# Edge attention over sorted edges: two small per-chunk tables kept on chip, and the broadcast row of relative node numbers carried as 16-bit floats

## What is computed

```python
q = (h @ Wq + bq).reshape(n, HD, HEADS) * scaling
k = (h @ Wk + bk).reshape(n, HD, HEADS)
v = (h @ Wv + bv).reshape(n, HD, HEADS)
s = jnp.einsum('edh,edh->eh', q[rows], k[cols])
m = jax.ops.segment_max(s, rows, num_segments=n)
e = jnp.exp(s - m[rows])
z = jax.ops.segment_sum(e, rows, num_segments=n)
attn = e / z[rows]
out = jax.ops.segment_sum(attn[:, None, :] * v[cols], rows, num_segments=n)
```

## Time and profile before

| | |
|---|---|
| median of 3 runs | 13238.97 us (13223.25 to 13242.68) |
| the profiled execution | 13243.9 us, its span 13242.3 us |
| PE busy | 6677.3 us (50%) |
| DVE busy | 6328.2 us (48%) |
| POOL busy | 6040.3 us (46%) |
| ACT busy | 2226.2 us (17%) |
| granted PE clock, mean | 0.736 |

### The profile page before, as it was taken

One profiled execution on the slowest core, in us unless ns is written; L12 is line 12 of the kernel. 1 busy time (PEld: TensorE's weight loads), 2 busy tenths in 40 slices (PEclk: granted clock), 3 DMA queues, 4 the chain that ended last, 5 costly groups with the idle time before them and its releaser, 6 DMA issues. The chain is left out here.

```text
span 13242.3 us, 124947 instructions
## 1 busy us (share of the span) xinstructions
PE 6677.3 (50%) x26695; PEld 4426.6 (33%) x26696; DVE 6328.2 (48%) x12364; ACT 2226.2 (17%) x4818; POOL 6040.3 (46%) x6038
## 2 busy tenths in 40 slices
PE   4647777777777659989996000000024200000399
PEld 2325555555555535555554000000013100000277
DVE  5855565656665757777777233333332100005133
ACT  1114444444443101111110000000000000000122
POOL 1215444444443045444444666666631477772300
PEclk8768898998998878998997555555555555555699
DMA  1136555555554211111112455545531111111100
GB/s 66 50 105 184 180 183 176 183 181 180 182 183 148 74 56 36 32 38 32 32 36 67 148 177 170 177 168 170 175 123 50 47 9 9 9 9 43 26 16 16
DMA packets 583830, 1307.39 MB, mean 99 GB/s; under 512 B 206400, under 2 KB 354069, under 8 KB 553239
## 3 DMA queue, kind: packets, MB, share of 16 engines
q0 software_dynamic: 296736, 704.79, 19.2%
q1 hardware_dynamic: 250581, 321.56, 7.2%
q10 hardware_dynamic: 36288, 278.41, 5.7%
HBM read 1001.64 MB, written 309.87 MB: 99 GB/s over the span
## 5 line engine op out<-in xcount | busy, mean ns | idle before, releaser
L965 POOL DMA_INDIRECT e_kv<-KV,e_idx x1712 | 1619.0, 946 | 1656.5 <-PE e_psA L1087 1141.1
L2304 POOL DMA_INDIRECT s_x<-XN,s_idx x1612 | 1555.7, 965 | 928.9 <-issue 520.7
L1592 POOL DMA_INDIRECT SD<-o_pay,o_pos x1024 | 1156.3, 1129 | 1191.4 <-DVEq L45 733.8
L2018 PE MATMUL psY_f<-w_f,H_f 128*128 128x512 f32 x3200 | 1457.2, 614 | 31.2 <-issue 31.2
L2546 POOL DMA_INDIRECT t_gr<-G,t_idx x1088 | 1131.9, 1040 | 362.7 <-issue 362.7
L2325 DVE SCALAR_TENSOR_TENSOR s_x<-s_x,s_same 128x256 f32<-128x256 f32 x1488 | 723.6, 486 | 1136.1 <-issue 992.9
L1309 PE MATMUL j_ps_s<-j_diag_s,ones 128*128 128x128 f32 x2 | 0.8, 502 | 2466.0 <-DVE j_diag_s L1272 2466.0
L1067 PE MATMUL e_psQ<-QA,e_oht 128*128 x3424 | 891.1, 406 | 193.4 <-issue 124.3
L1309 PE MATMUL j_ps_g<-j_diag_g,ones 128*128 128x128 f32 x2 | 0.8, 500 | 1790.5 <-DVE j_diag_g L1272 1790.5
L2018 PEld LDWEIGHTS psY_f<-w_f,H_f 128*128 128x128 f32 x3200 | 621.6, 197 | 788.7 <-issue 788.7
L1087 PE MATMUL e_psA<-QA,ident 128*128 x1712 | 659.4, 472 | 357.6 <-DVE QA L1199 182.5
(11 more groups left out here) (558 smaller groups left out, 12608.3 us busy)
## 6 DMA issues: line engine op xcount, KB each, us to landing
PS<-s_x ACTq DMA_DIRECT2D x124, 1664.0 KB
e_oht<-REL SPq DMA_DIRECT2D x107, 1024.0 KB
o_db<-in_L_ffn_edge_index_dram ACTq DMA_DIRECT2D x128, 512.0 KB
e_kv<-KV,e_idx POOLq DMA_INDIRECT x1712
s_x<-XN,s_idx POOLq DMA_INDIRECT x1612
hold<-T3D SPq DMA_DIRECT2D x107, 192.5 KB
t_gr<-G,t_idx POOLq DMA_INDIRECT x1088
SD<-o_pay,o_pos POOLq DMA_INDIRECT x1024
```

Source lines behind the costliest of these rows:

```text
L965: pool.indirect_dma_start(kv[:, s, t, :], None, k.KV, bass.IndirectOffsetOnAxis(ap=idx[:, s, t:t + 1], axis=0)).then_inc(kv_in[s][g], 16)
L1592: pool.indirect_dma_start(self.k.SD, bass.IndirectOffsetOnAxis(ap=self.pos[:, s, j:j + 1], axis=0), self.pay[:, s, j, :], None).then_inc(s ...
L2018: last = pe.matmul(psY[:, h, b, :], H[:, m, i * P:(i + 1) * P], w2[:, m, e:e + 2, :].rearrange("p e n -> p (e n)"), start=(m == 0), stop=( ...
L2304: pool.indirect_dma_start(x[:, s, j, :], None, k.XN2, bass.IndirectOffsetOnAxis(ap=idx[:, s, j:j + 1], axis=0)).then_inc(x_in[s], 16)
```

## The change

Three things change.

- `plan_steps` no longer writes SRCI and RELT to memory. The two transposed tables are made straight into tiles `src_i` and `relt` that live until `edge_attention` ends. POOL copies 16 columns of `src_i` into `idx` ahead of a chunk's first gather, ACT copies 16 columns of `relt` ahead of its one-hot of edges; each waits for its own copy.
- REL is cast to bf16 by DVE and stored so. The broadcast row is 512 KB per chunk.
- The row lands in a tile `relb` of its own with two slots. ACT reads it and writes `oht`, so SP's load waits for ACT's reading of the slot (`oht_abs`) and ACT waits for PE's use of `oht` (`q_ps`).

```diff
+        relb = sb("relb", [P, SC, STEP], BF16)
-        turned = sb("turned", [P, NSP, 2])
-        turned_i = sb("turned_i", [P, NSP, 2], I32)
+        turned, turned_i = (x[:].rearrange("p (s g) -> p s g", g=2) for x in (k.relt, k.src_i))
...
-            sp.wait_ge(lists_done, 2)
-            sp.dma_start(k.REL.rearrange("(c p) e -> p c e", p=P), rel[:]).then_inc(kept, 16)
+            sp.wait_ge(lists_done, 3)
+            sp.dma_start(k.REL.rearrange("(c p) e -> p c e", p=P), relb[:]).then_inc(kept, 16)
...
             sp.wait_ge(turn_sb, 2)
-            sp.dma_start(k.SRCI, turned_i[:].rearrange("p s g -> p (s g)")).then_inc(kept, 16)
-            sp.dma_start(k.RELT, turned[:].rearrange("p s g -> p (s g)")).then_inc(kept, 16)
-            sp.wait_ge(kept, 16 * 5)
+            sp.wait_ge(kept, 16 * 3)
...
             dve.wait_ge(lists_done, 1)
+            dve.tensor_copy(relb[:], rel[:]).then_inc(lists_done, 1)
             dve.tensor_tensor(T3[:, :, 1:P], d[:, :, 1:P], d[:, :, 0:P - 1], ALU.not_equal)
...
             def ahead(i, s):
-                at(sp, q_ps, i - 2, 4, 3)
-                sp.dma_start(oht[:, s, :], k.REL.rearrange("s e -> (s e)")[bass.ds(i * CT * P, CT * P)].partition_broadcast(P))\
+                at(sp, oht_abs, i - 2, 2, 1)
+                sp.dma_start(relb[:, s, :], k.REL.rearrange("s e -> (s e)")[bass.ds(i * CT * P, CT * P)].partition_broadcast(P))\
                     .then_inc(rel_in[s], 16)
-                at(sp, s_done, i - 2, 4, 3)
-                sp.dma_start(idx[:, s, :], k.SRCI[:, bass.ds(i * CT, CT)]).then_inc(idx_in[s], 16)
-                at(sp, oh_done, i - 2, 2, 1)
-                sp.dma_start(relt[:, s, :], k.RELT[:, bass.ds(i * CT, CT)]).then_inc(relt_in[s], 16)
...
             def gather(i, s):
-                loaded(pool, idx_in[s], i, s)
                 for g in range(4):
                     at(pool, agg_ps, i - 2, CS, 2 * g + 1)
+                    if g == 0:
+                        at(pool, s_done, i - 2, 4, 3)
+                        pool.tensor_copy(idx[:, s, :], k.src_i[:, bass.ds(i * CT, CT)]).then_inc(idx_done, 1)
+                        at(pool, idx_done, i, 1, 0)
...
                 if h == 0:
                     loaded(act, rel_in[s], i, s)
+                    at(act, q_ps, i - 2, 4, 3)
                 o = oht[:, s, h * HT:(h + 1) * HT]
-                act.activation(o, o, ACT.Abs, bias=k.negpart[:, 0:1]).then_inc(oht_abs, 1)
+                act.activation(o, relb[:, s, h * HT:(h + 1) * HT], ACT.Abs, bias=k.negpart[:, 0:1]).then_inc(oht_abs, 1)
...
                 if tiles[0] == 0:
-                    loaded(act, relt_in[s], i, s)
+                    at(act, oh_done, i - 2, 2, 1)
+                    act.activation(relt[:, s, :], k.relt[:, bass.ds(i * CT, CT)], ACT.Copy).then_inc(relt_done, 1)
+                    at(act, relt_done, i, 1, 0)
                     at(act, agg_ps, i - 2, CS, CS // 2 - 1)
```

More of the change, by code:

```diff
@@ L735, in _ @@
             for r in range(2):
-                pe.wait_ge(lists_done, 1 + 2 * r)
+                pe.wait_ge(lists_done, 1 + 3 * r)
                 if r:
@@ L867, in edge_attention @@
         oht = sb("oht", [P, 2, CT * P])
+        relb = sb("relb", [P, 2, CT * P], BF16)
         oh = k.hold[:, 0:2 * CT * P].rearrange("p (s t n) -> p s t n", s=2, t=CT)
@@ L886, in edge_attention @@
         set_done, table_in, q_in, zeroed = sem("set_done"), sem("table_in"), sem("q_in"), sem("zeroed")
-        rel_in, t3_in, flg_in, idx_in, relt_in = ([sem(f"{n}_in{s}") for s in range(2)] for n in (
-            "rel", "t3", "flg", "idx", "relt"))
+        rel_in, t3_in, flg_in = ([sem(f"{n}_in{s}") for s in range(2)] for n in (
+            "rel", "t3", "flg"))
         kv_in = [[sem(f"kv_in{s}_{g}") for g in range(4)] for s in range(2)]
@@ L895, in edge_attention @@
             "exp_done", "oht_done", "oh_done", "oht_abs", "oh_abs", "fac_done"))
-        x_step = sem("x_step")
+        x_step, idx_done, relt_done = sem("x_step"), sem("idx_done"), sem("relt_done")
         block = c.enter_context(nc.Block())
@@ L2739, in program @@
         k.SRCP, k.DSTP = scratch("SRCP", [NSUP * STEP], I32), scratch("DSTP", [NSUP * STEP], I32)
-        k.REL, k.T3D = scratch("REL", [NSP, STEP]), scratch("T3D", [2 * NSP, TW])
-        k.FLG, k.SRCI, k.RELT = scratch("FLG", [2 * NSP, 4]), scratch("SRCI", [P, 2 * NSP], I32), scratch("RELT", [P, 2 * NSP])
+        k.REL, k.T3D = scratch("REL", [NSP, STEP], BF16), scratch("T3D", [2 * NSP, TW])
+        k.FLG = scratch("FLG", [2 * NSP, 4])
         k.STEPB, k.STEPI, k.FIRST = scratch("STEPB", [NSP]), scratch("STEPI", [NSP], I32), scratch("FIRST", [NSP])
@@ L2772, in program @@
                 with ExitStack() as cw:
+                    k.relt = cw.enter_context(nc.sbuf_tensor("relt", [P, 2 * NSP], F32))
+                    k.src_i = cw.enter_context(nc.sbuf_tensor("src_i", [P, 2 * NSP], I32))
                     k.step_i, k.step_r = (cw.enter_context(nc.sbuf_tensor(n, [1, NSP], I32)) for n in ("step_i", "step_r"))
```

## The result

The kernel before took 13233.4 us (median of 11 runs), the changed one 13258.7 us (median of 11). The ratio is 1.0019, with a 95% interval of 1.0011 to 1.0027: 15 to 36 us slower. I had forecast 13227 us and a slight gain; the time lies inside the range, its sign was a rival's.

The account below looks back on a forecast made before the run. The loop was read as a chain of handovers, with PE's word late during POOL's gathers. Terms -4 - 16 + 21 + 13 - 26 = -12 on 13243.9 gave 13231.9, less 4.9 for the median: 13227 us, range 13075 to 13350.

Parts of the forecast that it names:

- POOL's term: Index copy ahead of each chunk's first gather: 0.5 us per chunk, a quarter counted, +13 us, bounds 0 and +54.
- POOL's copy sets the pace: Rival: slack in POOL's gather run is not real, every chunk 0.5 us longer; +55, 13294 us; 20 in 100.
- SP and the REL row: Loop: REL burst and small loads leave their place near L1101; -0.25 us per chunk, -26 us, bounds -170 and +107.
- ACT: Loop: node-column copy and wait, 0.4 us per chunk, on the path in half the chunks; +21 us, bounds 0 and +54.
- plan_steps: Part before edge_attention: both table stores go, DVE gets one more cast; -4 us, between -5.6 and +1.1.
- The start: Start of edge_attention: gathers begin without the idx load, so the first scan comes sooner; -16 us, bounds 0 and -20.
- The signs I had named: Loop: forecast wrong if L1161's wait falls well below 250 us, L1199's exceeds 400, or POOL's run of eight starts later.
- The last sign: Loop: forecast wrong if POOL's run of eight gathers starts later and everything after it does.
- The start of the chain: Loop: PE's finished word reaches others late during gather runs; DVE waits 343.3 us at L1161, 319.3 at L1199.

Follow-up runs that it names:

- e5: Kernel before with only the index columns kept in SBUF and copied by POOL ahead of the first gather: 13282.6 us, +29 to +66 us.
- e2: Changed kernel with ACT's copy moved a chunk earlier, to where ACT waits for PE: 13262.7 us, +19 to +48 against the kernel before.
- e3: Changed kernel with both POOL's and ACT's copies moved early, to where their engines wait: 13223.5 us, -15 to +16 against the kernel before.
- e4: Changed kernel with a second POOL copy and wait behind the first, ahead of the first gather: 13283.4 us, +40 to +77 against the kernel before.
- e1: Changed kernel with POOL's copy moved behind the last gather of the chunk before: 13238.0 us, -1 to +28 against the kernel before.
- e7: Kernel before with only the relative numbers in 16-bit floats in a tile of their own: 13220.1 us, -32 to -5 us.
- e6: Kernel before with only the node columns kept in SBUF and copied by ACT: 13249.1 us, +5 to +29 us.
- e10: Changed kernel with both copies early and POOL's run of eight gathers split into four, twelve following later: 13610.2 us, +270 to +316 against the kernel before.

## Why the prediction was wrong

**The step that failed** is POOL's term: "0.45, say 0.5 us per chunk ... I take a quarter", +13. Alone, the index part costs 48 us (29 to 66) although its start is earlier. The size of the copy was about right: with it the first gather is 0.58 us late, where I had 0.5. The quarter was wrong. I had taken it from a slack of 1.4 us in one run of eight gathers. Such a pause stood in 46 of 105 runs, and it took up 0.13 of the 0.58 us; of 0.52 to 0.58 us, 0.40 to 0.52 reach the stretch behind the run's end. In whole times it is 0.45 us per chunk of 0.58 in e5, 0.30 to 0.37 of 0.52 between e2 and e3, 0.23 to 0.31 of 0.29 in e4, and only 0.11 to 0.20 of 0.52 between the changed kernel and e1. So most of the copy is on the path, and my bound for that case, 107 x 0.5 = +54, is near the 48 us of e5. The rival "POOL's copy sets the pace" names the mechanism in the form in which it came ("the first gather of a chunk is late anyhow and the seven others are set by issue alone"), and I gave it 20 in 100; its price of +55 for the whole change was too high, 25 (15 to 36) came out. In what I expected of e1 and e4 I erred the other way: I took the 0.77 us that the page shows in front of a first gather for the copy's own price, and so 0.8 to 1.0 us where 0.58 and 0.29 were at stake.

**SP and the REL row**, -26: right in sign, wrong in place. Alone it gave 5 to 32 us, 4.5 us of it by the fourth scan, and nothing at L1161. I had doubts written beside it (the two late words are equally late, though only one has the load near it); e7 bears the doubt out.

**ACT**, +21: of the right size. The copy took 0.21 us and its wait 0.15 in the rows above, 0.36 where I had 0.4, and the stretch to the exponential is 0.24 to 0.35 us longer in the kernels that have it there; some 0.2 us come back behind it, so about half is on the path. Alone the part costs 17 us (5 to 29).

**plan_steps**, -4: -5.2 measured. **The start**, -16: the first scan is 12.1 us earlier with those 5.2 in it, so the start itself gave 7. I had written that the gathers beside the first loads could slow them, and they do: ACT's first REL row was in 11.6 us later than before, and of the single parts e5, with the early gathers and the old load, has that first wait at 131.2 us, e7, with the late gathers and the small load, at 114.7 (115.5 before). And the wait of 15.05 us in the earlier trace rows, from which I took most of this term, is much shorter in e6 and e7 (the fourth group starts at 998.6 and 996.2 us), whose gathers start nearly as late as before.

**The signs I had named.** I said I was wrong if the wait at L1161 fell well below 250 us, because then the burst mattered. It fell to 183 us and the burst did not matter (e5 has the burst, and there it falls to 149.9 + 30.7 = 181). The later run lets the word of the first small product (L1103) pass more often ahead of the run's end, and holds the fifth sum's. The last sign, "if POOL's run of eight starts later and everything after it does", is what the profile shows.

**The start of the chain was read rightly**: PE's words come late beside a run of gathers. e10 shows it by moving the run. What I had no way to see in one trace is that the same kernel also runs at a level where the words are prompt, and that the change's value differs with it: +25 us where words are late, 0 where they are prompt.

## What to carry to other kernels

A cheap copy that replaces a hidden load is not cheap where it stands first in a run: count how much later the run's first instruction starts (0.58 us here, of which most reached the loop), and put the copy where its engine waits anyway (the same change with both copies early cost nothing where the plain one lost 0.19%, and gained 0.6% where the plain one was even). A wait that shrinks need not be a gain: look for the one further down the chain that has grown. A gain of a few tenths of a percent wants to be measured at more than one level of the kernel before.

## What the runs showed of the hardware

- At the first two levels PE's completion words reach the others late while POOL issues gathers 1.25 us apart: the word that meets the end of a run arrives in the changed kernel 2.75 us after the start of its last gather, 1.7 to 3.2 us after the product, and with a run of twelve 9.8 us after it. At the third level, with the same program, they take 0.1 to 0.4 us, and the whole kernel is 8% faster (12187 against 13233 us). What sets the level is open; it doesn't go by the chip number of the record, which is 9 at two of them. Not every word inside a run is held: in the chunk of the changed kernel above, the first small product, L1103, starts at 2514.90 and DVE goes on with it at 2515.49, between two gathers.
- A first gather starts 0.78 us after the end of the product that it waits for, in the loop and with no copy between. A copy of 128x16 on POOL between them makes it 1.36 us, and a second one 1.65. From the end of the copy to the gather are 0.78 us in the 102 chunks whose copy stands in the body of the loop and 0.27 us (947.11 above) in the five whose copy stands outside of it, so most of the 0.78 isn't the wait for the result. In the loop there are register instructions between the two; that they take the time isn't shown. DVE's and ACT's own results are there after 0.17 and 0.15 to 0.2 us.
- Gathers issued beside the first REL load delay it: ACT's wait for it is 131.2 us in e5 and 126.5 in the changed kernel, where they are, and 114.7 in e7 and 115.5 in the kernel before, where they aren't.
- The change's effect on the step differs between the three levels: 0.46, 0.82 and 0.09 us longer, from one pair of profiles each.
